# A three-pass attention kernel: VectorE's work reordered, parts of it moved to ScalarE and GpSimd, and evictions split

## The reference

```python
# layer 0: pass 0 (attention with the mask, gate from ctx, MLP)
y = x + attn0(ln(x), mask) + (ctx @ Wg.T + bg)
y = y + relu(ln(y) @ W1.T + b1) @ W2.T + b2
# layer 1: pass 1 (causal self attention), pass 2 (cross attention with ctx, MLP)
z = y + mha(ln(y), ln(y), causal=True)
z = z + mha(ln(z), ctx, causal=False)
out = z + relu(ln(z) @ mlp_w1 + mlp_b1) @ mlp_w2 + mlp_b2
```

## Time and profile before

| | us |
|---|---|
| median of 3 runs | 1724.61 (1707.62 to 1731.74) |
| the profiled execution | 1704.09 |
| its span in the profile | 1702.3 |
| PE busy, matmuls | 1459.5 (86%) |
| DVE busy | 1212.1 (71%) |
| ACT busy | 1061.9 (62%) |
| POOL busy | 834.7 (49%) |
| granted PE clock over the span, 1 = 2.4 GHz | 0.956 |
| DMA: k_stack, q_stack reads | 288 issues of 128 KB each kind |

### The profile page before, as it was taken

How to read it: one execution, slowest core, us unless ns; L and a number is a source line. 1 busy time by engine, 2 the same in 40 slices (tenths; PEclk the granted TensorE clock), 3 DMA queues, 4 the chain that set the end, 5 groups by cost and what they waited for, 6 DMA issues and landing times.

```text
span 1702.3 us, 42833 instructions
## 1 busy us (share of the span) xinstructions
PE 1459.5 (86%) x13376; PEld 1175.9 (69%) x13376; DVE 1212.1 (71%) x3855; ACT 1061.9 (62%) x2153; POOL 834.7 (49%) x1125
## 2 busy tenths in 40 slices
PE   2789999999998998878787777778999999999986
PEld 1567788877777887765566555555777777777756
DVE  2688887888878887656666766666776777677742
ACT  3677676777777775445565555556656665666552
POOL 3345454444444566544344443444555655565533
PEclk8799999999999999989899999998999999999989
DMA  5645555444544455444655646574644364546300
GB/s 145 139 113 119 108 109 118 99 99 105 117 100 99 105 125 130 119 107 107 124 121 111 129 101 140 115 153 93 119 112 105 99 128 99 105 101 129 79 26 13
DMA packets 163511, 185.75 MB, mean 109 GB/s; under 512 B 15952, under 2 KB 140240, under 8 KB 163408
## 3 DMA queue, kind: packets, MB, share of 16 engines
q1 hardware_dynamic: 163408, 184.57, 49.8%
HBM read 125.78 MB, written 58.72 MB: 108 GB/s over the span
## 4 chain that ended last, share of the span: by engine, by line
PE 42%; issue 13%; ACT 12%; DVE 12%; DMA 9%; POOL 6%; SPq 5%; ACTq 1%; DVEq 0%; POOLq 0%
PE d_ps L437 16%; PE d_ps L673 8%; DMA k_stack<-parts 7%; PE o_ps L572 5%; PE s_ps L494 5%; PE t_ps L542 3%; DVE prob L858 3%; PE t_ps L508 3%; SPq L399 2%; DMA parts<-q_part 2%; ACT prob_t L721 2%; SPq L404 2%; DVE o_n L890 2%; POOL h_lo L1031 2%; PE m_ps L444 1%
## 5 line engine op out<-in xcount | busy, mean ns | idle before, releaser
L721 ACT ACTIVATE prob_t<-t_ps 128x384 f32<-128x384 f32 (+1 forms) x512 | 275.4, 551 | 393.0 <-PE t_ps L542 197.7
L494 PE MATMUL s_ps<-k_stack,q_stack 96*128 96x256 bf16 (+1 forms) x1536 | 294.6, 275 | 124.5 <-DMA k_stack<-parts 47.5
L712 ACT ACTIVATE prob<-prob,neg_max 128x256 f32<-128x256 f32 x512 | 233.8, 514 | 121.0 <-DVE neg_max L858 118.8
L494 PEld LDWEIGHTS s_ps<-k_stack,q_stack 96*128 96x128 bf16 x1536 | 115.1, 100 | 227.8 <-issue 65.7
L542 PE MATMUL t_ps<-q_stack,k_stack 108*128 108x256 bf16 (+1 forms) x1024 | 207.3, 269 | 23.0 <-ACT prob_t L721 14.3
L858 DVE CUSTOM_DVE_ANT_0 prob<-s_ps,bias_sb 128x256 f32<-128x256 f32 x512 | 192.4, 416 | 48.5 <-PE s_ps L494 36.7
L858 DVE CUSTOM_DVE_ANT_0 prob<-s_ps,causal 128x128 f32<-128x128 f32 (+1 forms) x512 | 158.5, 352 | 90.2 <-PE s_ps L494 88.0
L843 DVE TENSOR_REDUCE top<-s_ps 128x2 f32<-128x512 f32 x256 | 172.9, 682 | 54.8 <-PE s_ps L494 51.3
L1031 POOL TENSOR_TENSOR h_lo<-h_f,h_hi 128x512 fp32r<-128x512 f32 x128 | 165.9, 1296 | 86.6 <-DVE h_hi L921 86.6
L572 PE MATMUL o_ps<-prob_t,v_sb 128*17 128x256 f32 (+1 forms) x3072 | 200.7, 381 | 0.0
L437 PE MATMUL d_ps<-x2t_hi,w_hi 128*128 128x256 f32 x512 | 157.0, 307 | 38.2 <-ACT k_f L780 21.8
(11 more groups left out here) (115 smaller groups left out, 4063.5 us busy)
## 6 DMA issues: line engine op xcount, KB each, us to landing
q_stack<-parts SPq DMA_DIRECT2D x288, 128.0 KB, 4.0
k_stack<-parts SPq DMA_DIRECT2D x288, 128.0 KB, 6.4
parts<-q_part SPq DMA_DIRECT2D x96, 192.0 KB, 2.3
parts<-k_part SPq DMA_DIRECT2D x96, 192.0 KB, 2.3
ct_kept<-ct_hl SPq DMA_DIRECT2D x16, 512.0 KB, 8.0
x_in<-x_mid SPq DMA_DIRECT2D x32, 256.0 KB, 2.9
x_res<-x_mid SPq DMA_DIRECT2D x32, 256.0 KB, 3.0
ct_hl<-ct_kept SPq DMA_DIRECT2D x16, 512.0 KB, 8.2
```

Source lines behind the costliest of these rows:

```text
L494: last = mm(s_ps[:, h % 2, q * S:q * S + n], q_stack[0:ROWS, t.par, HEAD[h], q * P:(q + 1) * P], k_stack[0:ROWS, t.par, HEAD[h], 0:n], sta ...
L712: last = nc.scalar.activation(prob[:, h % 4, q, :], prob[:, h % 4, q, :], ACT.Exp, bias=neg_max[:, h % 4, q:q + 1], scale=-1.0)
L721: nc.scalar.activation(prob_t[:, h % 8, 0:n], t_ps[:, h % 2, 0:n], ACT.Exp, scale=-1.0)\
```

## The change

- **Minima first.** In DVE's slot, `score_guard` and the copy of transposed probabilities stand first instead of last.
- **First norm earlier.** Statistics, mean and normalising of `nxt2` move from slots 9, 10 and 12 to 4, 5 and 6 (`STATS_AT, MEAN_AT, HAT_AT`). In pass 0 `NORM_AT` goes from 6 to 7.
- **eps on POOL.** The addition of eps leaves DVE; POOL adds it ahead of its power, for the first norm now in slot 5, between its work on q and k there and its work in slot 6.
- **V by ACT** in passes 1 and 2, in one instruction of 128x512 instead of two of 128x256 on DVE.
- **float32 first, high part from it.** ACT evicts float32 once from PSUM, signals, waits for itself, and copies the high part from the float32 tile in SBUF, in one instruction. `k_done`, `q_done`, `xt_f` and so on come after the first; new events `k_p1`, `q_p1`, `xt_h`, `ct_h`, `x2t_h` after the second, and POOL waits for those.
- **No tile position for the minima.** `top_rows` uses a weight of 108 columns, of which the first 96 are zero, and writes rows 0 to 107.
- The causal mask is held once, as 128x256, and read at an offset.

```diff
-NORM_AT = (6, 10, 10)
+NORM_AT = (7, 10, 10)
+STATS_AT, MEAN_AT, HAT_AT = 4, 5, 6
...
                 for q in range(TT):
-                    last = mm(o_ps[ROWS:ROWS + TOP, S + q * P:S + (q + 1) * P],
-                              top_part[:, c % 2, q].rearrange("p j n -> p (j n)"), ident_bf[:, :],
-                              start=True, stop=True, tile_position=(0, ROWS))
+                    last = mm(o_ps[0:ROWS + TOP, S + q * P:S + (q + 1) * P], top_wide[:, c % 2, q, :], ident_bf[:, :],
+                              start=True, stop=True)
...
+            def high_part(task, dst, src, made, done):
+
+                act.wait_ge(made.sem, made.after(task))
+                act.sem_inc(passed, 1)
+                nc.scalar.activation(dst, src, ACT.Copy).then_inc(done.sem, 1)
...
                 if h == 4 and has(st.nxt):
                     act.wait_ge(k_mm.sem, k_mm.after(st.nxt))
...
+                        last = nc.scalar.activation(k_f[:, :, :], d_ps[:, 0, :].rearrange("p (m s) -> p m s", m=KC),
+                                                    ACT.Copy)
+                    last.then_inc(k_done.sem, 1)
+                    if st.cur:
                         act.wait_ge(k_written.of(st.cur), k_written.after(st.cur))
...
+                    high_part(st.nxt, k_part[:, 0], k_f[:, :, :], k_done, k_p1)
...
+                if h == V_AT + 1 and has(st.nxt, KEYED):
+                    act.wait_ge(v_mm.sem, v_mm.after(st.nxt))
+                    if st.prev:
+                        act.wait_ge(pv_mm.sem, pv_mm.after(st.prev))
+                    act.sem_inc(passed, 1)
+                    nc.scalar.activation(v_sb[:, st.nxt.par, :, :, 0:HD],
+                                         d_ps[:, 1, :].rearrange("p (k h d) -> p k h d", k=TT, d=HD), ACT.Copy)\
+                        .then_inc(v_done.sem, 1)
...
             def slot(st, h):
+                if has(st.cur):
+                    score_guard(st, h)
+                t, ht = head_at(st, h, LAG, (0,))
+                if t and ht % 2:
+                    dve.wait_ge(t_mm.sem, t_mm.after(t, ht + 1))
+                    ring_free(dve, st, t, ht)
+                    v.tensor_copy(prob_t[:, ht % 8], t_ps[:, 1, :]).then_inc(pt_odd.sem, 1)
...
-                if h == 9 and has(st.nxt2):
+                if h == STATS_AT and has(st.nxt2):
...
-                if h == 10 and has(st.nxt2):
+                if h == MEAN_AT and has(st.nxt2):
...
-                dve.wait_ge(mv_done.sem, mv_done.after(task))
-                v.tensor_scalar(ve_t[:, :], mv_t[:, :, 1], eps, None, ALU.add).then_inc(ve_done.sem, 1)
...
-                if h == 12 and has(st.nxt2):
+                if h == HAT_AT and has(st.nxt2):
...
                 if h == 5 and has(st.nxt):
-                    pool.wait_ge(k_done.sem, k_done.after(st.nxt))
+                    pool.wait_ge(k_p1.sem, k_p1.after(st.nxt))
                     sub(k_f[:, :, :], k_f[:, :, :], k_part[:, 0], k_r.sem)
...
-                if h == 10 and has(st.nxt2):
+                if h == MEAN_AT and has(st.nxt2):
+                    pool.wait_ge(ln_mv.sem, ln_mv.after(st.nxt2))
+                    pool.sem_inc(passed, 1)
+                    g.tensor_tensor(ve[:, :], mv[:, :, 1], eps_sb[:, st.nxt2.p], ALU.add).then_inc(ln_ve.sem, 1)
                     pool.wait_ge(ln_ve.sem, ln_ve.after(st.nxt2))
```

More of the change, by code:

```diff
@@ L594, in slot @@
                     weights(st.nxt, UNIT_QKV)
-                    pe.wait_ge(xt_f.sem, xt_f.after(st.nxt))
+                    pe.wait_ge(xt_h.sem, xt_h.after(st.nxt))
                     pe.wait_ge(xt_l.sem, xt_l.after(st.nxt))
@@ L730, in top_copies, with affine @@
                                      ACT.Copy).then_inc(top_row.sem, 1)
-            def affine(high, dst, col_g, col_b, done):
-                for out_t in (high, dst):
-                    for k in range(KC):
-                        last = nc.scalar.activation(out_t[:, k, :], m_ps[:, k * S:(k + 1) * S], ACT.Identity,
-                                                    bias=cols_sb[:, col_b + k:col_b + k + 1],
-                                                    scale=cols_sb[:, col_g + k:col_g + k + 1])
+            def affine(dst, col_g, col_b, done):
+                for k in range(KC):
+                    last = nc.scalar.activation(dst[:, k, :], m_ps[:, k * S:(k + 1) * S], ACT.Identity,
+                                                bias=cols_sb[:, col_b + k:col_b + k + 1],
+                                                scale=cols_sb[:, col_g + k:col_g + k + 1])
                 last.then_inc(done.sem, 1)
+            def high_part(task, dst, src, made, done):
+                act.wait_ge(made.sem, made.after(task))
+                act.sem_inc(passed, 1)
+                nc.scalar.activation(dst, src, ACT.Copy).then_inc(done.sem, 1)
             def slot(st, h):
@@ L936, in slot @@
                         dve.wait_ge(ln_rstd.sem, ln_rstd.after(st.nxt))
-                    aggregate(st.nxt2, stats, mv, ve, LN_EPS[st.nxt2.p], ln_stats, ln_mv, ln_ve)
-                if h == V_AT + 1 and has(st.nxt):
+                    aggregate(st.nxt2, stats, mv, ln_stats, ln_mv)
+                if h == V_AT + 1 and has(st.nxt, (0,)):
                     dve.wait_ge(v_mm.sem, v_mm.after(st.nxt))
@@ L987, in slot @@
                                     x2[:, st.old.par], ALU.add).then_inc(y_done.sem, 1)
-                if has(st.cur):
-                    score_guard(st, h)
-                t, ht = head_at(st, h, LAG, (0,))
-                if t and ht % 2:
-                    dve.wait_ge(t_mm.sem, t_mm.after(t, ht + 1))
-                    ring_free(dve, st, t, ht)
-                    v.tensor_copy(prob_t[:, ht % 8], t_ps[:, 1, :]).then_inc(pt_odd.sem, 1)
                 if st.s is not None:
@@ L1020, in _ @@
             g.memset(zeros[:, :, :], 0.0).then_inc(zeroed, 1)
-            pool.wait_ge(zeroed, 1)
+            g.memset(top_wide[:, :, :, :], 0.0).then_inc(zeroed, 1)
+            for p in range(NPASS):
+                g.memset(eps_sb[:, p], LN_EPS[p]).then_inc(zeroed, 1)
+            pool.wait_ge(zeroed, 2 + NPASS)
             pool.wait_ge(const_landed, 48)
@@ L1041, in top_split @@
                     pool.wait_ge(top_mm.sem, top_mm.after(before, cb + 1))
-                src, part = top[:, c % 2], top_part[:, c % 2]
+                src = top[:, c % 2]
+                part = top_wide[:, c % 2, :, ROWS:].rearrange("p q (j n) -> p q j n", n=NSPLIT)
                 g.tensor_tensor(part[:, :, :, 0], src, zeros[:, :, :], ALU.add).then_inc(top_1.sem, 1)
@@ L1096, in slot @@
                 if h == 14 and has(st.prev, MLP):
+                    pool.wait_ge(ln2_mv.sem, ln2_mv.after(st.prev))
+                    pool.sem_inc(passed, 1)
+                    g.tensor_tensor(ve2[:, :], mv2[:, :, 1], eps_sb[:, st.prev.p], ALU.add).then_inc(ln2_ve.sem, 1)
                     pool.wait_ge(ln2_ve.sem, ln2_ve.after(st.prev))
```

92 lines of the change are left out of this document (44 added, 48 removed).

## The result

The changed kernel takes **1851.39 us** (median of 4 runs, 1845.73 to 1852.56) against 1720.15 for the kernel before beside it: a ratio of **1.076 [1.067, 1.084]**, slower by about 131 us. The forecast was 1764, its range ended at 1795. The direction was right; the loss was 131 us where 39 were forecast. The profiled execution took 1845.73 us (span 1843.9).

What follows compares the result with a forecast made beforehand. PE bounds the kernel overall, with pass 1 limited by its k_stack loop and passes 0 and 2 close to PE's work. 24 + 15 + 0 = +39 us on 1724.6 gave 1764 us, range 1695 to 1795.

Steps and rivals of the forecast that it cites:

- +0.9 a step (from -1.0 ... to +1.8): Pass 0: DVE's new order makes each step 0.9 us longer, +15 us over 16 steps.
- So h_f is about 1.0 late, and V with it: Pass 0: work put ahead of DVE's second h_hi cast delays the last h_f and V product by about 1.0 us.
- The 0.4 and 1 us taken as coming back: Pass 0: ot_hi now behind the cast returns some 0.4 us, POOL's ot_lo no longer ahead of h_lo about 1.
- The normalising of nxt2 (2 x 0.46 = 0.9): Pass 0, DVE: two normalising instructions now ahead of the second h_hi cast, counted at 0.9 us of the 2.4 added.
- The wait of 0.98 for a minimum stays: Pass 0: guard 0 then stands behind the second norm and the store's addition, so the 0.98 us wait is unchanged.
- Pass 1, +1.5 a step: Pass 1: +0.7 minima first, +0.2 high part from SBUF, +0.6 eps and power on POOL; +24 us over 16 steps.
- k_part behind the power: Pass 1, POOL: eps and power ahead of k_part send the k parts out 1.0 us later, +0.6 after 0.4 hidden.
- The other 0.7, top_rows of slot 2 behind the turn: Pass 1, slot 2: the turn of o_ps follows the minimum, so top_rows starts later, +0.7 us a step (0.5 to 0.8).
- More for k_stack: Pass 1, a sign of being right: more PE waits for k_stack and fewer for top L858.
- Rival C: Longer k_stack waits in pass 1 lower PE's clock, +15 us; with pass 0 at its upper end 1793 us; chance 0.10.
- 0.0 a step: Pass 2: top_rows' delay and the returns cancel, 0.0 us a step (-0.6 to +0.8).
- top_rows' +1.0 and +0.5: Pass 2: top_rows starts later behind minimum and turn, +1.0 us in slot 10 and +0.5 in slot 2.

Runs made afterwards that it cites:

- e1: Kernel before with only DVE's minima and copy of transposed probabilities moved first in the slot: 1816.22 us, 1.059.
- e3: Changed kernel with the first norm back in slots 9, 10 and 12 and NORM_AT 6 in pass 0: 1799.84 us, 1.050.
- e2: Kernel before with only the first norm moved to slots 4, 5 and 6, eps still added on DVE: 1754.72 us, 1.022.
- e7: Kernel before with the minima first in all slots except 13 to 15: 1776.74 us, 1.032.
- e9: Kernel before with the first norm's statistics, mean and power early, but its normalising left in slot 12: 1720.82 us, 1.004.
- e12: Kernel before with only V of passes 1 and 2 evicted by ACT and eps added by POOL: 1708.77 us, 0.996.
- e11: Kernel before with only the minima's tile position removed (weight of 108 columns, causal mask held once): 1715.78 us, 1.000.
- e10: Kernel before with only float32 evicted first and the high part copied from it in SBUF: 1704.93 us, 0.992.
- e8: Kernel before with four spare copies on ACT ahead of each MLP's last h_f eviction: 1783.91 us, 1.041.

## Why the prediction was right or wrong

- **Pass 0, "+0.9 a step (from -1.0 ... to +1.8)": the step that failed.** "So h_f is about 1.0 late, and V with it": the wait for h_f rose by 2.2 (26.7 - 4.8 over ten), and minima first alone makes all of it (26.8 in e1, 28.3 in e3, 5.4 in e2). The sum counted each minimum ahead of the casts at its bare length (0.8) and put the wait of DVE for the scores under it at nothing. In e1 that wait is 2.29 us in slot 6, and it goes on through DVE's k_part, POOL's k_part and h_lo to the third h_f. The 0.4 and 1 us taken as coming back did not come. "The normalising of nxt2 (2 x 0.46 = 0.9)" was mis-sized too, 2.55 measured, since it meets POOL's k_part and ct_hl, though the prediction had read just such a blocked cast in the earlier trace rows and used it in pass 1 alone; but its price in pass 0, 1.8 a step alone, is not paid in h_f.
- **"The wait of 0.98 for a minimum stays": wrong.** It rose to 1.3, with an x_hat wait of 1.0 beside it; e7 prices the place at 2.0 us a step, nearly all of it as PE busy longer. The chain was in the text (guard 0 behind the second norm and the store's addition), but 2.4 us of x_hat and y on DVE between the minima of heads 15 and 0 were given no price, nor was PE's wait for x_hat behind guards 14 and 15. DVE's pause of 1.17 us where its loop turns is no part of the error: the kernel before has it at the same place.
- **Pass 1, +1.5 a step: seen in part, and its size is in part luck.** k_part behind the power is as forecast, and the stretch from K's first eviction to q_stack is 1.0 longer, 0.8 forecast. The other 0.7, top_rows of slot 2 behind the turn, is not seen: POOL's last part releases top_rows there, and the waits for the turn lie in slots 6, 10 and 14. "More for k_stack" did not come either; that wait fell from 29.0 to 9.3 us. And a step of pass 1 is no constant: in the profile of before the steps run from 24.5 to 31.1 us, and the shortest, three of 24.5, are the only ones at clock 1.00 among the twelve from 758 on; the others lie between 25.3 and 31.1 at 0.87 to 0.94. The 27.0 of the earlier trace rows belongs to an execution 12 us under the median of 32 later ones; e9 to e12 average 27.6 to 28.4. Against these the changed kernel's 28.6 is +0.2 to +1.0. In it the steps are alike (27.7 to 29.3), most at 0.85 to 0.93.
- **The clock, a term missing from passes 0 and 2.** Rival C had it, in pass 1 only, at 1.5 us a step. It was placed where the clock was already low; it showed most where it had been 1.00 over the windows and had most to lose: PE busy 2.8 us a step longer in pass 0, 1.1 in pass 2. In pass 2 that is too low a figure for the clock, since without the tile position the same matmuls are busy 0.7 a step less (e11). In pass 0 it is an upper end, since a fall of the clock there can be taken up by waits: the third step of the kernel before in its window has 0.96 and is 39.8 us long, like the others beside it at 1.00 (39.5 to 39.9). Over the kernel PE's busy time grew by 56 us, more than the whole forecast loss.
- **Pass 2, "0.0 a step": wrong.** top_rows' +1.0 and +0.5 came nearly as read (0.70 and 0.56 waited for o_q, 11.3/9 = 1.3 us a step; minima first alone +1.1 a step), and so did the 0.5 back from k_f (7.0 to 2.9 over nine steps). What was to come back beside it did not: the wait for a minimum fell by 0.1, not 0.4 (3.2 to 2.6), and that for probabilities rose (6.7 to 7.5). Left out: the normalising in slot 6 ahead of the high parts of this pass too, 0.8 a step alone by e2 and gone in e9; V's wait for h_f went from nothing to 1.2 a step. With both orders in, the clock falls as well.
- **k_f first, "nothing":** 0.3 a step in pass 0 and 0.6 in pass 2 by e10. **Tile position**, taken at 0.1: 0.2 of PE's time at each top_rows, nothing in the kernel's time; the prediction's "close to PE's own work" does not hold for pass 2. **V and eps**, nothing except 0.4 in pass 2: 0.7 there, at the edge.
- **The range.** Its upper end put pass 0 at its worst and the clock in pass 1. Even with every term of idle time right (2.2, 1.2 and 2.0 a step, 86 us) it would have ended near 1810; PE's longer busy time is the rest.
- What stays open: why the small parts are worth 26 us on the old orders and nothing with the early norm (that eps on POOL lengthens the wait of the normalising for its power was not tried alone); what sets the step of 34.0 in pass 2; and in which steps the clock falls when the waits are the same in all. The clock was never changed by itself: that it costs time is shown by the equal steps of pass 2, and its share in the changed kernel is only bounded by PE's busy time.

## What to carry to other kernels

Where PE's granted clock is 1.00, price a new wait on PE higher than its length: in e8 a wait of 1.6 us a step cost 3.0 in pass 0 and 1.2 or 2.8 in pass 2, as the clock held or fell behind it. The clock has most to take in the stretch where it is full. When an instruction is moved on DVE, look at what POOL runs at the new place, and at what is queued behind: here two instructions of 0.46 became 2.55. In an order written by hand, waiting for the newest result first delays all older work that is ready: DVE stood idle for 2.29 us for new scores, and POOL and ACT behind it for 2.75 and 2.67. And a wait that names an engine is no proof that the engine's work is what bounds: in pass 2 PE got 0.7 us a step shorter and the step did not.
